# Eight early loads moved from step 4 to step 3, and two GpSimd copies moved behind a root

## The chip, the cores and the metric

The kernel runs on one core of a Trainium2 chip. The metric is the device time of one execution in microseconds (us). Times before the change come from three executions; one more execution was recorded by the hardware profiler. All places in time below are in us from the start of the profiled span.

## The reference, cut to what matters

Two decoder layers on `x` (16 sequences x 100 tokens x 256). Each sub-layer is added to the running rows:

```python
x = x + L0_attn(layernorm(x))              # a state-space mixer with an MLP      -> stage "mixer"
x = x + L0_xattn(layernorm(x), ctx, ctx)   # cross attention, 16 heads, 361 keys  -> stage "cross0"
x = x + L0_ffn(layernorm(x))               # 32 experts, 4 per token              -> stage "cross0"
x = x + L1_attn(layernorm(x))              # self attention                       -> stage "layer1"
x = x + L1_xattn(layernorm(x), ctx, ctx, mask)                                  # -> stage "layer1"
x = x + L1_ffn(layernorm(x))               # 8 experts, 1 per token               -> stage "experts1"
```

In the cross attention the queries are `(x Wq + bq)` and the keys `(ctx Wk + bk)`, split into 16 heads of 16. The kernel writes each of them as three bfloat16 parts (first, rest, third), so that a bfloat16 product of a stack of 96 rows keeps float32 precision.

## The kernel before

**Four stages with a barrier of all engines between them.** The first, `stage_mixer`, works in four steps, `n = 1` to `4`; a step holds four sequences. Beside the mixer and its MLP each step computes the key parts of both cross attentions for its four sequences: eight units, `u = 0` to `7`, with even `u` for layer 0. A unit is a projection on TensorE, a bias on ScalarE, and three parts by turns of ScalarE and VectorE; SyncE (SP) stores the parts to DRAM (`k_stack`, line 511). The queries of step `n - 1` are computed in step `n` and stored at `u == 6` (`store_queries`, line 487, `q_stack`). Those of step 4 are left to the next stage.

**The order on each engine is written out by hand.** Each engine has its own program of waits and instructions and runs it strictly in order. On SP, step `n` is: the stores of units 0 to 5, then `front(n + 1)`, the load of the next step's rows (line 474, into `mixer_xg`), then the stores of the queries, then units 6 and 7, then the store of the step's result (line 517, which waits for `v_out`). On VectorE the next step's `front` (two layer norms, lines 542 to 555) stands between the third part of unit 5 and the rest of unit 7, and the last thing in a step is the addition of the MLP's result (line 738), which increments `v_out`. TensorE waits for `v_out` and for the front's result before it turns the next step's rows (line 936).

**The first heads.** Cross attention starts with sequence 0. Its queries and keys are loaded ahead, during the mixer, by `first_heads` (lines 490 to 501): for each of two halves of the heads one load of queries (`ctx_first_q`) and three of keys (`ctx_first_k`), eight in all, on SP's queue. The semaphore of slot 0 of the key stores counts units 0 and 4 of every step.

**The start of the second stage,** `stage_cross_experts`. TensorE computes scores of sequence 0 (line 2579), VectorE takes their maxima (line 3026), and from then on TensorE works through sequences `b` and, in each, through twelve units `k`. Work of the queries of the mixer's step 4 is spread over `b == 0` and `b == 1`: VectorE's moments (lines 3198 to 3205) at `k == 0`, the inverse root on GpSimd (line 3375), VectorE's normalisation at `k == 4` (line 3210, four instructions, increments `q_norm`), TensorE's turn at `k == 6` and `7` (line 2714), which waits for `q_norm`. GpSimd first copies the selector rows of the keys (line 3365) into three buffers, then makes `base` for sequence 0 (line 3336), then the root, then `base` for sequence 1. TensorE waits for two of the three copies at `b == 2` and for all at `b == 3`.

Of the kernel before, what the change touches and what calls it, by code (L numbers as in the profile page):

```python
# [28 lines left out]
NG = B // G  # L29
# [3 lines left out]
KD = D // P  # L33
# [67 lines left out]
Q_PARTS = [(0, 0, 3), (1, 3, 5), (2, 5, 6)]  # L101
# [240 lines left out]
def stage_mixer(prog):  # L342
# [9 lines left out]
    UNITS = G * len(LAYERS)  # L352
    with stage(nc, "mixer") as (sem, sbuf, psum):
# [24 lines left out]
        keys_stored = [sem(f"keys_stored{s}") for s in range(4)]  # L378

        q_stats, q_mean, q_var, g_root, q_norm = (sem(n) for n in ("q_stats", "q_mean", "q_var", "g_root", "q_norm"))  # L380
        pe_qt, a_qt, pe_q, a_q, q_part1, q_rest_set, q_part2, q_part3, q_stored = (
            sem(n) for n in ("pe_qt", "a_qt", "pe_q", "a_q", "q_part1", "q_rest_set", "q_part2", "q_part3", "q_stored"))
# [49 lines left out]
        def out_rows(n):  # L432

            return prog.x2[:, (n - 1) * G:n * G, :] if n == NG else xo[:]
# [10 lines left out]
        def earlier(engine, semaphore, n, per=1):  # L445

            if not (isinstance(n, int) and n == 1):
                engine.wait_ge(semaphore, n * per - per)
# [17 lines left out]
        def group(dram, n):  # L466
            return dram[bass.ds((n - 1) * G, G)].rearrange("g t d -> t g d")

        with nc.Block() as block:
            @block.sync  # L470
            def _(sp):
                def front(n):
                    earlier(sp, x_free, n)
                    sp.dma_start(xg[:], group(x_dram, n)).then_inc(x_in, 16)
                    if n == 1:
                        prog.load_segment(sp, 0)
                        prog.load_segment(sp, 1)
                        prog.load_segment(sp, 2)
                        sp.dma_start(prog.consts[:], prog.ins["consts"]).then_inc(consts_in, 16)
                        prog.load_segment(sp, 3)  # L480

                def store_queries(n):
                    sp.wait_ge(q_part3, n)
                    for m in range(KD):
                        for k, at, end in Q_PARTS:
                            places = prog.q_stack[0][m, at:end, :, (n - 1) * G:n * G].rearrange("g p b t -> p g (b t)")
                            sp.dma_start(places, q_part[:, k, m].unsqueeze(1).broadcast_to(places.shape)
                                         ).then_inc(q_stored, 16)

                def first_heads():  # L490
                    sp.wait_ge(q_stored, (NG - 2) * KD * len(Q_PARTS) * 16)
                    sp.wait_ge(keys_stored[0], (NG - 1) * UNITS // 4 * 16)
                    for h in range(2):
                        sp.dma_start(prog.ctx_first_q[0:SHIFT_ROW, h, 0:HH * T].rearrange("p (h n) -> p h n", h=HH),
                                     prog.q_stack[0][h, :, :, 0:1].rearrange("g (d h) b t -> (g d) h (b t)", h=HH)
                                     ).then_inc(prog.ctx_first_in[h], 16)
                        for at, end in K_PARTS:
                            sp.dma_start(prog.ctx_first_k[at * DH:end * DH, h, 0:HH * S2]
                                         .rearrange("p (h n) -> p h n", h=HH),
                                         prog.k_stack[0][0, 0:end - at, :, h].rearrange("k (d h) n -> (k d) h n", h=HH)  # L500
                                         ).then_inc(prog.ctx_first_in[h], 16)

                def step(n, n_next):
                    if n == NG:
                        first_heads()
                    for u in range(UNITS):
                        if u == 6 and n > 1:
                            store_queries(n - 1)
                        layer, l = LAYERS[u % 2][0], u % 2
                        wait_unit(sp, v_part3, n, u)  # L510
                        sp.dma_start(prog.k_stack[layer][bass.ds(n * G + (u // 2 - G), 1)]
                                     .rearrange("b k p m n -> p (b k) (m n)"),
                                     part[u % 4][:].rearrange("p k m n -> p k (m n)")).then_inc(keys_stored[u % 4], 16)
                        if u == 5 and n_next is not None:
                            front(n_next)
                    sp.wait_ge(v_out, n)
                    sp.dma_start(group(out_dram, n), out_rows(n)).then_inc(out_stored, 16)

                run(sp, front, step)
                sp.wait_ge(q_stored, (NG - 1) * KD * len(Q_PARTS) * 16)  # L520
                sp.wait_ge(out_stored, 16 * NG)
                sp.wait_ge(rest_in, 16)
                sp.wait_ge(consts_in, 16)
                for s in range(4):
                    sp.wait_ge(keys_stored[s], B * len(LAYERS) // 4 * 16)
# [1740 lines left out]
def stage_cross_experts(prog):  # L2266
# [35 lines left out]
    with stage(nc, "cross0") as (sem, sbuf, psum):  # L2302
        def pair(label):
# [10 lines left out]
        consts_set, heads_set, third_heads_set = sem("consts_set"), sem("heads_set"), sem("third_heads_set")  # L2314
        q_stats, q_mean, q_var, g_root, q_norm = (sem(n) for n in ("q_stats", "q_mean", "q_var", "g_root", "q_norm"))
        pe_qt, a_qt, pe_q, a_q, q_part1, q_rest_set, q_part2, q_part3, q_stored = (
            sem(n) for n in ("pe_qt", "a_qt", "pe_q", "a_q", "q_part1", "q_rest_set", "q_part2", "q_part3", "q_stored"))
# [150 lines left out]
        with nc.Block() as block:  # L2468
# [862 lines left out]
            def _(g):  # L3331
# [32 lines left out]
                def select_heads(r, h):  # L3364
                    nc.gpsimd.tensor_copy(by_head(k_sb[r][:, h] if r < 2 else third_k, S2)[SHIFT_ROW:P],
                                          prog.c("head_sel")[SHIFT_ROW:P, h * HH:(h + 1) * HH].unsqueeze(2)
                                          .broadcast_to([32, HH, S2])).then_inc(third_heads_set, 1)

                for i, (r, h) in enumerate(((0, 0), (2, 1), (0, 1))):
                    select_heads(r, h)  # L3370
                    g.wait_ge(third_heads_set, i + 1)
                g.wait_ge(v_bias, 1)
                set_base(0)
                g.wait_ge(q_var, 1)
                nc.gpsimd.tensor_tensor(q_root[:], q_width[:], prog.half_neg[0:T, :], ALU.pow).then_inc(g_root, 1)
                g.wait_ge(g_root, 1)
                for b in range(B):
                    if b + 1 < B:
                        set_base(b + 1)
                    if b == 2 * G:  # L3380
                        g.wait_ge(zeroed, 16)
                    if b >= 2 * G:
                        scatter(b // G - 2, b % G * TOPK, TOPK // 2)
                    if b > 0:
                        root(b - 1)
                        inverse_length(b - 1)
                    if b >= 2 * G:
                        scatter(b // G - 2, b % G * TOPK + TOPK // 2, TOPK // 2)
# [267 lines left out]
```

## Time and profile before

| | |
|---|---|
| time, median of three | 1659.65 us (1657.05 to 1666.83) |
| the profiled execution: its own time | 1666.83 us |
| its span, first to last instruction | 1664.7 us |
| mean granted TensorE clock | 0.952 of full speed |
| mixer stage, about | 0 to 264 us of the span |
| second stage begins | 268.7 us |

The span and the profiled execution's own time differ by 2.1 us, which lies around the instructions. TensorE is busy for 89% of the span. The profile's rows of single engines in order of time give start, duration, engine and line, what is written from what, the number of instructions merged into the row, and in brackets the idle time before it with what ended it. SPq is the queue of SP: its rows are the issues of transfers, not the transfers.

### The profile page before, as it was taken

What the parts mean: (1) busy time and instruction counts of PE and PEld (TensorE: products, weight loads), DVE (VectorE), ACT (ScalarE), POOL (GpSimd) and SP (SyncE); (2) the same over time, 40 slices, a digit from 0 to 9 for tenths busy, and PEclk for the clock granted to TensorE, in tenths of its full rate; (3) what the DMA queues carried; (4) which work ended last, traced back from release to release, by engine and by line L of the source; (5) the groups of instructions that cost most, each with busy time, mean ns of one, the idle gap of its engine ahead of it and who ended that gap; (6) DMA issues with size and microseconds to landing.
All of it is one profiled execution on the core that took longest, in us unless ns stands there. A gap on an engine that the chain in (4) does not pass through costs nothing. (4 is left out here: it accounts for less than half of the span.)

```text
span 1664.7 us, 30297 instructions
## 1 busy us (share of the span) xinstructions
PE 1487.7 (89%) x11672; PEld 1119.9 (67%) x11672; DVE 790.6 (47%) x2238; ACT 701.7 (42%) x1473; POOL 479.4 (29%) x428
## 2 busy tenths in 40 slices
PE   6999997998888999999999957898799999939996
PEld 3666664666665668888888824565466667629885
DVE  6577574567765422222222246765566666541111
ACT  3464464666666112222222234456656555502221
POOL 2122122011334536666666420111111111012332
PEclk9999997999999999999999977999899999959998
DMA  7343556697772217777777527357477776339995
GB/s 300 121 146 97 159 163 111 122 171 125 127 132 60 61 40 196 201 199 194 196 195 195 137 48 168 85 111 148 93 143 128 122 134 120 67 110 328 325 297 151
DMA packets 252439, 250.86 MB, mean 151 GB/s; under 512 B 116724, under 2 KB 226700, under 8 KB 246796
## 3 DMA queue, kind: packets, MB, share of 16 engines
q1 hardware_dynamic: 210316, 221.13, 52.7%
q0 software_dynamic: 41984, 27.84, 9.9%
q8 instruction: 93, 1.52, 0.4%
q14 instruction: 46, 0.38, 0.1%
HBM read 194.10 MB, written 54.58 MB: 149 GB/s over the span
## 5 line engine op out<-in xcount | busy, mean ns | idle before, releaser
L2831 PE MATMUL cross_ps_score<-cross_q,cross_k 128*128 128x250 f32 x1024 | 223.5, 376 | 0.8 <-DVE cross_q L3312 0.8
L2831 PEld LDWEIGHTS cross_ps_score<-cross_q,cross_k 128*128 128x128 f32 x1024 | 195.5, 191 | 23.9 <-DVE cross_q L3312 1.0
L3321 DVE TENSOR_TENSOR cross_prob<-cross_act_,cross_ps_score 128x250 f32<-128x250 f32 x128 | 53.2, 416 | 268.3 <-ACT cross_act_ L2999 268.3
L3412 POOL DMA_INDIRECT x_sum<-cross_ye,cross_token x64 | 128.6, 2009 | 80.9 <-ACT cross_ye L3005 68.7
L1745 ACT ACTIVATE layer_parts<-layer_ps_prob 128x400 f32<-128x400 f32 (+1 forms) x192 | 97.0, 508 | 106.4 <-PE layer_ps_prob L1561 103.9
L3026 DVE TENSOR_REDUCE cross_nmax<-cross_ps_score 100x2 f32<-100x722 f32 x128 | 112.1, 903 | 61.8 <-PE cross_ps_score L2579 61.5
L2861 ACT ACTIVATE cross_prob<-cross_ps_prob 128x400 f32<-128x400 f32 (+1 forms) x192 | 96.3, 508 | 87.6 <-PE cross_ps_prob L2612 86.8
L2999 ACT ACTIVATE cross_act_<-cross_ps_score 128x250 f32<-128x250 f32 x128 | 48.6, 380 | 167.6 <-PE cross_ps_score L2831 167.6
L2843 PE MATMUL cross_ps_prob<-cross_val,cross_prob 128*125 128x256 f32 x512 | 115.8, 379 | 0.0
L3587 ACT ACTIVATE experts_h<-experts_ps_h,experts_b 128x128 f32<-128x128 f32 x160 | 45.7, 368 | 138.8 <-PE experts_ps_h L3556 138.8
L3402 POOL DMA_INDIRECT cross_xe<-ln_rows,cross_token x64 | 79.6, 1244 | 81.7 <-PE cross_ps_misc L2817 57.5
L2843 PEld LDWEIGHTS cross_ps_prob<-cross_val,cross_prob 128*125 128x125 f32 x512 | 93.5, 188 | 12.8
L928 PE MATMUL mixer_bank<-mixer_ctx,packed_sb 128*128 128x361 f32 x256 | 86.4, 481 | 2.5 <-ACT xt L832 2.2
L1967 DVE CUSTOM_DVE_ANT_0 packed_sb<-layer_ps_score,layer_mask 100x361 bf16<-100x361 f32 x128 | 63.0, 532 | 39.1 <-PE layer_ps_score L1518 38.7
L3005 ACT ACTIVATE cross_ye<-cross_ps_prob,cross_weight 125x256 f32<-125x256 f32 x64 | 26.9, 471 | 111.4 <-PE cross_ps_prob L2843 111.4
L1967 DVE CUSTOM_DVE_ANT_0 packed_sb<-layer_ring,layer_mask 100x361 bf16<-100x361 f32 x128 | 62.7, 528 | 22.7 <-PE layer_ring L1518 22.7
L3361 POOL DMA_INDIRECT row_token<-cross_choice,cross_row_put x64 | 64.3, 1005 | 31.6 <-issue 14.0
L928 PEld LDWEIGHTS mixer_bank<-mixer_ctx,packed_sb 128*128 128x128 f32 x256 | 48.8, 195 | 30.3 <-issue 5.3
L1556 PE MATMUL layer_ps_prob<-consts_sb,layer_mask 100*128 100x400 bf16 x192 | 64.5, 336 | 3.9 <-ACT layer_parts L1745 1.1
L813 ACT ACTIVATE mixer_full<-mixer_bank,packed_sb 128x361 f32<-128x361 f32 x64 | 34.8, 561 | 78.0 <-PE mixer_bank L928 76.2
L1561 PEld LDWEIGHTS layer_ps_prob<-layer_m_q,layer_stacks 128*128 128x128 bf16 x720 | 51.9, 98 | 23.1
L3522 POOL DMA_INDIRECT out<-experts_ye,experts_put x20 | 31.7, 1586 | 114.2 <-DMA out<-experts_ye,experts_put 103.2
(471 smaller groups left out, 3111.1 us busy)
## 6 DMA issues: line engine op xcount, KB each, us to landing
packed_sb<-in_w SPq DMA_DIRECT2D x20, 1024.0 KB, 7.0
experts_w<-in_w SPq DMA_DIRECT2D x20, 1024.0 KB
k_stack<-mixer_part SPq DMA_DIRECT2D x32, 541.5 KB, 3.9
cross_k<-in_wg SPq DMA_DIRECT2D x32, 512.0 KB, 5.4
cross_k<-in_wu SPq DMA_DIRECT2D x32, 512.0 KB, 6.9
cross_val<-in_wd SPq DMA_DIRECT2D x32, 512.0 KB, 5.2
layer_stacks<-k_stack SPq DMA_DIRECT2D x30, 270.8 KB, 5.3
cross_k<-k_stack SPq DMA_DIRECT2D x25, 270.8 KB
```

What stands on the lines that cost most here:

```text
L928: ins = nc.tensor.matmul(bank[6 + m][:, 0:S2], prog.w(f"{LAYERS[l][1]}_wk", KD)[:, k, m * P:(m + 1) * P], ctx[s][:, k, :], start=(k == 0), ...
L1556: nc.tensor.matmul(ps_prob[k % 2][:, 0:GT], mask[b % M_BUFFERS][:, at:at + P], prog.c("tile_diag")[0:T, :], start=True, stop=False)
L1745: nc.scalar.activation(m_prob_sb[0:rows_, q4 % 2, t, :], ps_prob[k % 2][0:rows_, 0:GT], ACT.Exp, scale=DH ** -0.5).then_inc(m_prob, 1)
L1967: ins = nc.vector.tensor_tensor_reduce(m_scratch[:, h % HH, :], m_score[(u % 2) * 2 + j][0:T, 0:S2], mask[b % M_BUFFERS][:, 0:S2], -1.0, - ...
L2831: ins = nc.tensor.matmul(ps_pre[m][:, side, 0:CAP], w[s][:, k, m * P:(m + 1) * P], xt[s][:, k, :], start=(k == 0), stop=(k == KD - 1))
L2843: ins = nc.tensor.matmul(ps_sum[s][0:HALF, t, :], up[s][:, m, t * HALF:(t + 1) * HALF], wd[s][:, m, :], start=(m == 0), stop=(m == NUP - 1))
L2861: nc.scalar.activation(prob[0:rows_, q4 % 2, t, :], ps_prob[k % 2][0:rows_, 0:GT], ACT.Exp, scale=DH ** -0.5).then_inc(a_prob, 1)
L3026: nc.vector.tensor_reduce(nmax[b % 2][:, 2 * u:2 * u + 2], ps_score[0:T, (u % 2) * 2:(u % 2) * 2 + 2, 0:S2], AX.X, ALU.max, negate=True).t ...
L3321: nc.vector.tensor_tensor(up[s][:, m, :], act_[:, m % 2, :], ps_pre[m][:, 1, 0:CAP], ALU.mult).then_inc(v_gated[m][s], 1)
L3361: g.indirect_dma_start(prog.row_token, bass.IndirectOffsetOnAxis(row_put[:, c:c + 1], 0), choice[:, c, :], None).then_inc(scattered, 16)
L3402: g.indirect_dma_start(xe[s][:, t, :], None, prog.ln_rows, bass.IndirectOffsetOnAxis(token[:, 2 * e + t:2 * e + t + 1], 0)).then_inc(rows_ ...
L3412: g.indirect_dma_start(prog.x_sum, bass.IndirectOffsetOnAxis(token[:, 2 * e + t:2 * e + t + 1], 0), ye[s][:, t, :], None, compute_op=ALU.a ...
```

## The change

It does two things. In the mixer, `first_heads` is called in step 3 right behind the store of unit 3, instead of at the beginning of step 4, and waits for smaller counts of the same two semaphores. In the second stage, GpSimd copies selector rows into one buffer before the root and into the two others behind it.

```diff
                 def first_heads():
-                    sp.wait_ge(q_stored, (NG - 2) * KD * len(Q_PARTS) * 16)
-                    sp.wait_ge(keys_stored[0], (NG - 1) * UNITS // 4 * 16)
+                    sp.wait_ge(q_stored, KD * len(Q_PARTS) * 16)
+                    sp.wait_ge(keys_stored[0], 5 * 16)
                     for h in range(2):
...
                 def step(n, n_next):
-                    if n == NG:
-                        first_heads()
                     for u in range(UNITS):
                         if u == 6 and n > 1:
                             store_queries(n - 1)
...
                         if u == 5 and n_next is not None:
                             front(n_next)
+                        if u == 3 and n == 3:
+                            first_heads()
...
-                for i, (r, h) in enumerate(((0, 0), (2, 1), (0, 1))):
-                    select_heads(r, h)
-                    g.wait_ge(third_heads_set, i + 1)
+                select_heads(0, 0)
+                g.wait_ge(third_heads_set, 1)
                 g.wait_ge(v_bias, 1)
                 set_base(0)
                 g.wait_ge(q_var, 1)
                 nc.gpsimd.tensor_tensor(q_root[:], q_width[:], prog.half_neg[0:T, :], ALU.pow).then_inc(g_root, 1)
                 g.wait_ge(g_root, 1)
+                select_heads(2, 1)
+                g.wait_ge(third_heads_set, 2)
+                select_heads(0, 1)
+                g.wait_ge(third_heads_set, 3)
                 for b in range(B):
```

## Rows read from the trace of the kernel before

**Rows 1.** The head of the page.
```profile
span 1664.7 us, 30297 instructions
```
**Rows 2.** In order of time, SP: the stores that end steps 2, 3 and 4.
```profile
141.91 0.30 SPq L517 DMA_DIRECT2D x_after<-mixer_xo  x1
...
202.40 0.30 SPq L517 DMA_DIRECT2D x_after<-mixer_xo  x1
...
262.88 0.30 SPq L517 DMA_DIRECT2D x_after<-packed_sb  x1
```
**Rows 3.** In order of time, SP: first and last of the eight loads, and the next store.
```profile
202.82 0.69 SPq L494 DMA_DIRECT2D ctx_first_q<-q_stack  x1
...
208.61 1.96 SPq L498 DMA_DIRECT2D ctx_first_k<-k_stack  x3
216.44 21.96 SPq L511 DMA_DIRECT2D k_stack<-mixer_part  x6
```
**Rows 4.** In order of time, SP, step 3: stores of units 2 and 3, and the row load.
```profile
169.81 2.02 SPq L511 DMA_DIRECT2D k_stack<-mixer_part  x2
...
177.97 0.42 SPq L474 DMA_DIRECT2D mixer_xg<-in_x  x1
```
**Rows 5.** In order of time, VectorE, step 3: front's start, last part, last addition.
```profile
183.67 1.41 DVE L542 BATCH_NORM_STATS2 mixer_stats<-mixer_xg 100x6 f32<-100x256 f32 x4 [5.23 <-DMA mixer_xg<-in_x]
...
195.97 0.91 DVE L537 TENSOR_TENSOR mixer_part<-mixer_rest,mixer_part 128x722 bf16<-128x722 f32 x1 [0.86 <-ACT mixer_part L825]
201.09 1.29 DVE L738 TENSOR_TENSOR mixer_xo<-mixer_bank,mixer_base 100x512 f32<-100x512 f32 x2 [4.21 <-PE mixer_bank L1023]
```
**Rows 6.** Stretches: length, busy PE, PEld, DVE, ACT, POOL, clock, DMA share, GB/s.
```profile
142.00:150.00 8.00, 7.97 (x36) 5.59 (x37) 4.60 (x8) 2.48 (x4) 0.00 (x0) 1.00 0.19 53
172.00:178.00 6.00, 6.00 (x19) 3.42 (x18) 4.28 (x6) 5.28 (x9) 0.60 (x1) 1.00 0.80 263
178.00:183.30 5.30, 5.30 (x18) 3.10 (x17) 0.44 (x1) 1.74 (x3) 0.00 (x0) 1.00 0.90 255
202.40:215.40 13.00, 12.88 (x55) 9.03 (x56) 9.23 (x21) 5.24 (x9) 1.40 (x2) 1.00 0.88 142
273.00:293.00 20.00, 16.66 (x126) 10.43 (x126) 14.74 (x39) 9.69 (x17) 6.22 (x5) 0.67 1.19 153
```
**Rows 7.** SP's issues at the second stage's start, and the landing time of one at 283.56.
```profile
269.56 0.58 SPq L2473 DMA_DIRECT2D cross_q<-q_stack  x1
...
276.90 0.59 SPq L2482 DMA_DIRECT2D cross_src<-in_ctx_t  x1
...
cross_src<-in_ctx_t SPq DMA_DIRECT2D x1, 361.0 KB, 11.2
```
**Rows 8.** In order of time, GpSimd (POOL): third copy, base 0, root, base 1.
```profile
274.08 2.59 POOL L3365 COPY cross_k<-consts_sb 32x2888 bf16<-32x2888 bf16 x1
279.56 0.73 POOL L3336 TENSOR_TENSOR cross_base<-cross_xin,cross_bias_sum 100x256 f32<-100x256 f32 x1 [2.89 <-issue]
284.30 1.01 POOL L3375 TENSOR_TENSOR cross_q_root<-cross_q_width,half_neg 100x4 f32<-100x4 f32 x1 [4.01 <-DVE cross_q_width L3205]
287.84 0.87 POOL L3336 TENSOR_TENSOR cross_base<-cross_xin,cross_bias_sum 100x256 f32<-100x256 f32 x1 [2.53 <-DMA cross_xin<-x_after]
```
**Rows 9.** VectorE's SBUF-to-SBUF instructions beside GpSimd's; base: min/median/max ns.
```profile
287.08 1.78 DVE L3210 TENSOR_SCALAR packed_sb<-packed_sb,cross_q_mv,cross_q_root 100x256 f32<-100x256 f32 x4
288.05 0.81 DVE L3210 TENSOR_SCALAR packed_sb<-packed_sb,cross_q_mv,cross_q_root 100x256 f32<-100x256 f32 x1
164.66 2.35 POOL L796 TENSOR_TENSOR mixer_base<-mixer_base,packed_sb 100x1024 f32<-100x1024 f32 x1
164.71 2.46 DVE L555 TENSOR_SCALAR mixer_xh<-mixer_x,mixer_mv,mixer_rstd 100x256 f32<-100x256 f32 x1 [0.93 <-POOL mixer_rstd L753]
L3336 POOL TENSOR_TENSOR cross_base<-cross_xin,cross_bias_sum x16: 725/728/867, 279.6 to 518.0; 100x256 f32<-100x256 f32 x16
```
**Rows 10.** In order of time, TensorE's turn of the queries; then a stretch, as in group 6.
```profile
288.92 0.93 PE L2714 MATMUL cross_ps_misc<-packed_sb 100*128 100x100 f32 x4 [1.43 <-DVE packed_sb L3210]
...
284.90:295.10 10.20, 8.77 (x83) 5.98 (x72) 6.91 (x11) 3.71 (x8) 1.28 (x2) 0.50 1.13 161
```

## The prediction

> **What bounds the kernel now.** I read the page first, then the two places that the change touches, each engine in order of time. The span is 1664.7 us [rows 1] and the profiled execution took 1666.83 us, so 2.1 us lie around it; it is the slowest of the three, 7.2 us above the median of 1659.65. My sum is a difference against this execution, and I put the difference on the median. A busy share for the whole span says nothing about 25 us of it. What counts is who waits last at four places: SP's queue at the start of step 4, the row load in step 3, GpSimd at the start of the second stage, and TensorE's wait for the normalised queries.
>
> **What the removal of the loads from step 4 is worth.** The eight loads are issued from 202.82 to 208.61 + 1.96 = 210.57, 7.75 us, and SP's next store is issued at 216.44 [rows 3], because its data comes only then. So SP has 5.9 us to spare, and nobody waits behind the loads. A second sign: the steps end at 141.91, 202.40 and 262.88 [rows 2]. Step 3, without the loads at its start, took 60.49 us, and step 4, with them, 60.48. The gain is 0. The transfers themselves lie in the stretch that ends at 215.4 [rows 6], and the first heads are first used when the second stage begins, at 268.7, so earlier data is worth 0 too.
>
> **What the insertion into step 3 costs.** The store of unit 3 is issued by 169.81 + 2.02 = 171.83 [rows 4]; the loads then stand before the stores of units 4 and 5 and, above all, before the load of the next step's rows, now issued at 177.97. Both new waits are met by then: the queries of step 1 were stored in step 2, and unit 0 of step 3 is stored before units 1 to 3. VectorE stands idle for 5.23 us for exactly this row load and starts at 183.67 [rows 5]. Any delay D of its landing moves the whole front. What hides it: VectorE's last part in this step ends at 195.97 + 0.91 = 196.88, and its next instruction waits 4.21 us for TensorE [rows 5]. Behind that wait the path is tight, since the addition releases the next step on TensorE. So the cost is D - 4.2 where D is over 4.2, and 0 otherwise.
>
> D by issue alone: with 7.75 us of issuing the loads end at 171.83 + 7.75 = 179.6, two stores follow, taken at the row load's 0.42 each [rows 4], and the row load goes out at 180.4, so D is at least 2.4.
>
> D by transfer work: I count a DMA share times its stretch. From 202.4 to 215.4 it is 13.0 x 0.88 = 11.4; the 400 KB store that opens that stretch costs 8.0 x 0.19 = 1.5 in the stretch where it is alone [rows 6]. The eight loads are therefore 9.9 us of work. In step 3 the DMA engines already do 6.0 x 0.80 + 5.3 x 0.90 = 9.6 from 172 until the rows have landed. Together 19.5. At a share of 1.0 this ends at 191.5, D = 8.2; at the 1.19 that these engines reach when they are full [rows 6], at 172 + 16.4 = 188.4, D = 5.1. I take the middle, D = 6.6: a cost of 2.4 us.
>
> The upper end comes from the second stage, where the same kind of load fills the engines. Eight half-loads there take 269.56 to 276.90, 7.3 us, and a 361 KB load issued behind them took 11.2 us to land [rows 7]. If our issuing stretches by 3 us and the landing takes 11.2, the rows land at 180.4 + 3 + 11.2 = 194.6, D = 11.3, a cost of 7.1. The lower end is 0.
>
> The Trainium skill says in "DMA: Bandwidth & Descriptors", section "Issuing engines are not separate DMA queues", that transfers of all issuing engines run on the same 16 DMA engines and interleave. By that, the stores and GpSimd's context load in the same stretch also compete with the row load, which is the assumption behind adding all work up; by issue alone the cost would be 0.
>
> **What the new order on GpSimd gives.** The third copy ends at 274.08 + 2.59 = 276.67, and GpSimd then waits 2.9 us before base 0, and 4.01 us on VectorE before the root [rows 8]. With one copy only it would be free some 5 us sooner and wait for the same two things. The gain is 0: neither base nor root comes earlier.
>
> **What the new order costs.** The two copies now start right behind the root, which ends at 284.30 + 1.01 = 285.31 [rows 8]. The first runs from about 285.4 to 288.0, the second would follow at once. VectorE's four instructions of the normalisation start at 287.08 [rows 9], in the middle of it. Three of them take 288.05 - 287.08 = 0.97 us, 0.32 each. The trace shows twice what happens when such an instruction meets a running GpSimd one. At 164.71 VectorE's took 2.46 us and ended at 167.17, just behind the GpSimd instruction of 164.66 to 167.01. At 288.05 the fourth took 0.81, while base 1 ran from 287.84 to 288.71 and was itself longer than its median of 0.73 [rows 8, 9]: GpSimd came in between the third and the fourth and made the fourth wait, although VectorE had more to do.
>
> So: the first waits until 288.0 and runs to 288.3. Then, as at 288.05, GpSimd's next instruction comes in, now a copy of 2.59 and not a base of 0.73, until 290.9. The other three end at 290.9 + 1.0 + 0.1 = 292.0. Today the normalisation ends at 287.08 + 1.78 = 288.86. The difference is 3.1 us. If VectorE keeps its turn and runs all four behind the first copy, they end at 289.4, a cost of 0.5. If the copies blocked nothing, base 1 would no longer be in the way, a gain of 0.4. I take 3.1, since the only row where a GpSimd instruction waits among these four shows it cutting in.
>
> Who waits: TensorE's turn of the queries starts at 288.92 after 1.43 us of idling for this very result [rows 10], and everything behind it on TensorE is in order. I see no later wait of that size in which the delay could vanish. Base 1, now about 4 us later, is needed only in sequence 1's result, and the copies only at `b == 2`, long after 291.
>
> The Trainium skill, in "SBUF — State Buffer", section "Who interferes with whom", says that GpSimd and a VectorE instruction that uses two ports hold a shared pair of ports exclusively for a whole instruction. The trace agrees, with 2.46 us instead of 0.4. It is the rule that speaks against this change; without it the second half would give the 0.4.
>
> **Sum.** 0 + 2.4 + 0 + 3.1 = +5.5 us. In the profiled execution's terms 1672.3, on the median 1659.65 + 5.5 = 1665.2 us. That is 0.33%, below the 0.5% (8.3 us) at which a measurement of this kernel can tell a difference.
>
> **The rivals.**
>
> A. Both delays are hidden. D stays under 4.2, since the rows' transfer work need not wait for all of the stores' work, and VectorE keeps its turn: 0 + 0.5, 1660.2 us. For it: D's floor by issue is 2.4. Against: 9.9 us of added work in a stretch already 80 to 90% full.
>
> B. The queue fills, and this ends on the slower side: the row load lands as slowly as the load of 11.2 us [rows 7]. It decides from D = 9.4, where 5.2 + 3.1 reaches 8.3. At D = 11.3 it is 7.1 + 3.1 = +10.2, 1669.9 us. Against it: in the second stage the queue had been full for much longer.
>
> C. TensorE's clock moves. From 284.9 to 295.1 it has 0.50 of full speed, 1.2 GHz, with 8.77 us busy [rows 10]; it fell after a stretch with pauses. If the rise stays where it is while the work moves 3.1 us later, 3.1 us of half-speed work run at full speed, a return of 1.5. If the longer pause adds a further half-speed stretch of like length, half of its 8.8 busy us are lost, 4.4. Against the sum: 1663.7, or 1669.6 us.
>
> D. The loads at step 4's start cost something that I don't see, a gain; rows 2 bound it at nothing, so only chance in clocks elsewhere could make it show.
>
> **How the numbers follow.** Both costs about as forecast, 1661.5 to 1668: 0.52. A: 0.23. B: 0.10. C: 0.11. D or a lucky set of clocks: 0.04. All of A, nearly all of the first and most of C lie within 0.5%. Slower by over 0.5% is B with a few points of C, of the first and of the scatter: 0.15. Faster: 0.04. Within: 0.81. The range runs from A less the scatter seen below the median, 2.6 us (1657.6, say 1658), to B's 1669.9 (1670).
>
> **What the profile after would show.** The eight loads issued from about 171.9; the row load of step 4 issued near 180 to 183, VectorE's wait for it about 12 us instead of 5.23; the end of step 3 not at 202.40 but near 204.8; step 4 again 60.5 long. In the second stage, counted from its start, one normalisation instruction of about 1.2 us and one of about 2.9, and TensorE's wait before its turn of 4.5 instead of 1.43. The prediction is wrong if step 3 keeps its 60.5 us, if the second copy waits until the four instructions are through, or if a later wait shrinks by what the turn was late.

## The result, and the profile after

| | before | changed |
|---|---|---|
| median of ten runs | 1662.80 us | 1671.86 us |
| lowest and highest | 1657.05, 1671.44 | 1668.22, 1685.03 |
| profiled execution, its span | 1666.83, 1664.7 | 1678.71, 1676.6 |
| mean granted clock | 0.952 | 0.953 |

The ratio over paired runs is 1.0069, 95% interval 1.0048 to 1.0092: slower by 0.69%, or 11.5 us (8.0 to 15.3). The two medians of ten differ by 9.1 us; over all 26 recorded executions of the changed kernel the median is 1674.9 us, 12.1 above 1662.80. The forecast was +5.5 us and 1665.2, with 1670 as the upper end.

**Step 3 of the mixer.** SP in order of time, from the end of step 2 to the end of step 4. SPq rows are issues.
```profile
142.06 0.30 SPq L517 DMA_DIRECT2D x_after<-mixer_xo  x1
156.10 15.88 SPq L509 DMA_DIRECT2D k_stack<-mixer_part  x4
172.09 0.69 SPq L494 DMA_DIRECT2D ctx_first_q<-q_stack  x1
172.83 3.07 SPq L498 DMA_DIRECT2D ctx_first_k<-k_stack  x3
175.94 0.77 SPq L494 DMA_DIRECT2D ctx_first_q<-q_stack  x1
176.75 3.07 SPq L498 DMA_DIRECT2D ctx_first_k<-k_stack  x3
179.86 1.48 SPq L509 DMA_DIRECT2D k_stack<-mixer_part  x2
181.38 0.81 SPq L474 DMA_DIRECT2D mixer_xg<-in_x  x1
...
205.76 0.30 SPq L517 DMA_DIRECT2D x_after<-mixer_xo  x1
...
267.93 0.30 SPq L517 DMA_DIRECT2D x_after<-packed_sb  x1
```
The eight loads stand where the four rows from 172.09 to 179.82 are. The row load goes out at 181.38 instead of 177.97 [rows 4]. Step 3 takes 205.76 - 142.06 = 63.70 us and step 4 62.17, against 60.49 and 60.48 [rows 2].

VectorE in order of time: the first part of `front`, its last part of the step, and the addition.
```profile
191.33 1.41 DVE L542 BATCH_NORM_STATS2 mixer_stats<-mixer_xg 100x6 f32<-100x256 f32 x4 [12.75 <-DMA mixer_xg<-in_x]
...
203.63 0.91 DVE L537 TENSOR_TENSOR mixer_part<-mixer_rest,mixer_part 128x722 bf16<-128x722 f32 x1 [0.86 <-ACT mixer_part L825]
204.46 1.28 DVE L738 TENSOR_TENSOR mixer_xo<-mixer_bank,mixer_base 100x512 f32<-100x512 f32 x2
```
The wait is 12.75 us where it was 5.23 [rows 5], so D is 7.5. The addition has no idle time ahead of it any more. The 4.21 us that covered the delay [rows 5] are used up, and the rest, 7.5 - 4.2 = 3.3, is what step 3 is longer by (3.2).

TensorE in order of time at the beginning of step 4, then two stretches in the columns of group 6.
```profile
205.88 0.88 PE L936 MATMUL mixer_bank<-packed_sb,mixer_xh 100*128 100x100 f32 x8 [3.48 <-DVE mixer_xo L738]
206.60 2.34 PE L928 MATMUL mixer_bank<-mixer_ctx,packed_sb 128*128 128x361 f32 x4
208.73 3.65 PE L971 MATMUL mixer_bank<-mixer_xt,packed_sb 128*128 128x400 f32 x8
```
```profile
206.90:210.30 3.40, 3.40 (x7) 1.91 (x6) 0.59 (x1) 1.88 (x3) 0.00 (x0) 0.50 0.50 139
295.70:302.50 6.80, 4.37 (x42) 3.22 (x43) 4.11 (x5) 1.49 (x3) 1.82 (x2) 0.50 0.55 71
```
TensorE stood idle for 3.48 us, and right behind it the granted clock is 0.50, 1.2 GHz instead of 2.4, for 3.40 us in which TensorE is busy throughout. Work of 3.4 us at half speed would take 1.7 at full speed, and 1.7 us is what step 4 is longer by. The forecast has nothing of this.

**The second stage.** It begins at 273.80, 5.05 us later. GpSimd, VectorE and TensorE in order of time. The four normalisation instructions stand first as one row and then one by one.
```profile
290.48 1.01 POOL L3374 TENSOR_TENSOR cross_q_root<-cross_q_width,half_neg 100x4 f32<-100x4 f32 x1 [5.15 <-DVE cross_q_width L3205]
291.56 2.59 POOL L3365 COPY packed_sb<-consts_sb 32x2888 bf16<-32x2888 bf16 x1
294.21 2.59 POOL L3365 COPY cross_k<-consts_sb 32x2888 bf16<-32x2888 bf16 x1
296.88 0.72 POOL L3336 TENSOR_TENSOR cross_base<-cross_xin,cross_bias_sum 100x256 f32<-100x256 f32 x1
```
```profile
292.74 5.34 DVE L3210 TENSOR_SCALAR packed_sb<-packed_sb,cross_q_mv,cross_q_root 100x256 f32<-100x256 f32 x4
292.74 1.56 DVE L3210 TENSOR_SCALAR packed_sb<-packed_sb,cross_q_mv,cross_q_root 100x256 f32<-100x256 f32 x1
294.22 2.73 DVE L3210 TENSOR_SCALAR packed_sb<-packed_sb,cross_q_mv,cross_q_root 100x256 f32<-100x256 f32 x1
296.88 0.88 DVE L3210 TENSOR_SCALAR packed_sb<-packed_sb,cross_q_mv,cross_q_root 100x256 f32<-100x256 f32 x1
297.68 0.40 DVE L3210 TENSOR_SCALAR packed_sb<-packed_sb,cross_q_mv,cross_q_root 100x256 f32<-100x256 f32 x1
```
```profile
298.13 0.93 PE L2714 MATMUL cross_ps_misc<-packed_sb 100*128 100x100 f32 x4 [5.37 <-DVE packed_sb L3210]
```
Lay the first two fences beside each other. The first normalisation waits for the end of the first copy (294.15), the second for the end of the second (296.80), the third for the end of base 1 (297.60); only the fourth has its own length. Each GpSimd instruction that is waiting comes in between two of VectorE's. Together they take 5.34 us, against 1.78 before [rows 9]. TensorE's wait is 5.37, against 1.43 [rows 10].

**The account.** TensorE's first product of sequence 1's probabilities starts at 310.61 in this profile and at 302.29 in that of before, 8.3 us later: 5.05 from the mixer and the rest from this wait, partly given back by the granted clock, which is 0.50 for 6.8 us at the place where it was 0.50 for 10.2 [rows 10]. The spans differ by 11.9 us. The largest further part is in the tenth to fifteenth sequences of the second stage, each of which is 0.6 to 2.6 us longer here, 6.5 together, of which shorter stretches elsewhere give back about 3. In the one that is 2.6 us longer TensorE's granted clock was 0.50 from 452.7 for 6.8 us, with 6.6 busy, and in the profile of before it was 1.00 throughout. What the rest is, is one of the questions of the experiments.

### The profile page after: what moved, and what is told of

It is laid out like the page before. It is cut to its first block and busy times, and to the rows that moved or that the text cites. A ratio compares the mean times of both kernels' runs of the same rounds, so it can differ in the third digit from the quotient of the medians.

```text
span 1676.6 us, 30297 instructions
## 1 busy us (share of the span) xinstructions
PE 1492.7 (89%) x11672; PEld 1122.4 (67%) x11672; DVE 793.3 (47%) x2238; ACT 701.1 (42%) x1473; POOL 480.3 (29%) x428
## 5 line engine op out<-in xcount | busy, mean ns | idle before, releaser
L928 PEld LDWEIGHTS mixer_bank<-mixer_ctx,packed_sb 128*128 128x128 f32 x256 | 49.8, 199 | 31.0 <-issue 6.5
```

Source lines behind the costliest of these rows:

```text
L928: ins = nc.tensor.matmul(bank[6 + m][:, 0:S2], prog.w(f"{LAYERS[l][1]}_wk", KD)[:, k, m * P:(m + 1) * P], ctx[s][:, k, :], start=(k == 0), ...
```

## The experiments

Every run is beside runs of the kernel before on the same chip. Their median was 1664.16 us in the group of the first four experiments (35 runs), 1672.11 in that of the next four (23 runs, another chip) and 1670.26 in a third group, a single run.

### e1: the loads alone

The eight loads in step 3 with the smaller counts, GpSimd's order as before.
```diff
+                        if u == 3 and n == 3:
+                            first_heads()
```


> The kernel before with the first half of the change alone: the eight loads behind unit 3's store in step 3; GpSimd's copies as before. Theory (row load late, then clock): VectorE waits about 12.7 us for the rows of step 4 as in the changed kernel, step 3 is 3.2 us longer than 60.5, TensorE stands idle for about 3.5 us before its turn and part of step 4 runs at half clock, 1.7 us more; the second stage begins 5.0 us late and its first sequence is as long as before. About +5 us in all. Rival (the two halves need each other, or the 9 us are scatter of the clock elsewhere): the second stage begins within 1 us of before, or it begins 5 us late and the time is nevertheless unchanged.

Measured: median 1671.30 us, ratio 1.0039 (1.0018 to 1.0061). VectorE's and TensorE's rows in order of time:
```profile
192.95 1.41 DVE L542 BATCH_NORM_STATS2 mixer_stats<-mixer_xg 100x6 f32<-100x256 f32 x4 [13.01 <-DMA mixer_xg<-in_x]
```
```profile
207.50 1.20 PE L936 MATMUL mixer_bank<-packed_sb,mixer_xh 100*128 100x100 f32 x8 [3.74 <-DVE mixer_xo L738]
```
Step 3 takes 63.96 us, step 4 62.15. Both parts of the mixer's loss come with the loads: 3.5 us by the late rows and 1.7 by the clock, which is at 0.50 from 207.9 for 3.4 us.

### e2: the copies alone

```diff
-                for i, (r, h) in enumerate(((0, 0), (2, 1), (0, 1))):
-                    select_heads(r, h)
-                    g.wait_ge(third_heads_set, i + 1)
+                select_heads(0, 0)
+                g.wait_ge(third_heads_set, 1)
...
+                select_heads(2, 1)
+                g.wait_ge(third_heads_set, 2)
+                select_heads(0, 1)
+                g.wait_ge(third_heads_set, 3)
```


> The kernel before with the second half of the change alone: two of GpSimd's copies behind the root; the eight loads as before. Theory (shared port): VectorE's four normalising instructions take about 5.3 us instead of 1.8, TensorE's wait before the turn of the queries is 4.5 to 5.4 us instead of 1.4, and sequence 1 begins 3 us late; mixer unchanged. About +3 us in all. Rival (a clock effect): the four instructions take 1.8 us and the time moves only by where TensorE's half-speed stretch falls. Open in both: whether the ten later sequences of the second stage get longer, as in the changed kernel (0.9 us each from the tenth on).

Measured: median 1668.38 us, ratio 1.0030 (1.0007 to 1.0053). All mixer steps take 60.5 us. TensorE in order of time:
```profile
293.81 0.93 PE L2714 MATMUL cross_ps_misc<-packed_sb 100*128 100x100 f32 x4 [5.36 <-DVE packed_sb L3210]
```
The same wait as in the whole change, without the loads; VectorE's four instructions take 5.36 us. From the first product of the second stage to TensorE's first product of sequence 1's probabilities it is 37.5 us here, and 36.8 and 36.0 in the two profiles of the changed kernel. In the nine profiles in which no late copy stands ahead of the normalisation and the moments are where they were, it is 31.4 to 33.5: the copies cost about 4 us there, and one profile alone can't tell that to better than 2, since the half-speed stretches of this stage fall differently from one execution to the next. The two parts add up: 0.39% + 0.30% is the 0.69% of the whole. Each has an interval of 0.2% to either side, so a sum that agrees to the hundredth is partly luck.

### e3 and e4: each half moved behind the instruction that it delays

e3 has the loads two units later, at `u == 5`, right behind the row load. e4 has the two copies wait for the normalisation.
```diff
+                        if u == 5 and n == 3:
+                            first_heads()
```
```diff
                 g.wait_ge(g_root, 1)
+                g.wait_ge(q_norm, 1)
+                select_heads(2, 1)
```


> As e1, but the eight loads stand in step 3 behind the load of the next step's rows (at unit 5) instead of ahead of it. Theory (the order on SP's queue is what costs): VectorE's wait for the rows is 5 to 6 us as before, step 3 is 60.5 us, the second stage begins within 0.5 us of before; no change in time. Rival (contention of the DMA engines, whatever the order): the rows still land 2 us or more late, since transfers of one queue interleave; with under 4.2 us of delay step 3 would still be 60.5 us, but the wait would show it.

> As e2, but the two late copies wait in addition until VectorE has normalised the queries. Theory (shared port): the four instructions take 1.3 us, 0.5 less than before, since base 1 is no longer in their way either; TensorE's wait before the turn is 0.9 to 1.4 us; time as before or 0.4 us less. Rival (any late copy costs, by base 1 coming late or by slowing other VectorE work): sequence 1 still begins 1 us or more late.

Measured: e3 median 1664.38 us, ratio 1.0001 (0.9976 to 1.0026); e4 1666.13 us, 1.0005 (0.9979 to 1.0031). VectorE in e3, then GpSimd, VectorE and TensorE in e4, each in order of time:
```profile
186.99 1.41 DVE L542 BATCH_NORM_STATS2 mixer_stats<-mixer_xg 100x6 f32<-100x256 f32 x4 [6.40 <-DMA mixer_xg<-in_x]
```
```profile
291.11 2.59 POOL L3365 COPY packed_sb<-consts_sb 32x2888 bf16<-32x2888 bf16 x1 [2.71 <-DVE packed_sb L3210]
```
```profile
289.60 1.38 DVE L3210 TENSOR_SCALAR packed_sb<-packed_sb,cross_q_mv,cross_q_root 100x256 f32<-100x256 f32 x4
```
```profile
291.03 0.56 PE L2714 MATMUL cross_ps_misc<-packed_sb 100*128 100x100 f32 x4 [1.37 <-DVE packed_sb L3210]
```
The same transfers in the same step, issued behind the row load, delay it by 1.2 us (6.40 against 5.23; the five other profiles with this part of the mixer unchanged have 5.22 to 5.59, so every D here is good to about 0.4), and the idle time ahead of the addition hides that: steps 3 and 4 take 60.5. The same copies behind the normalisation leave it at 1.38 us. So it is neither the work that costs nor the stage it stands in, but what it stands ahead of. The removals are worth nothing that can be measured: e3 has the loads gone from step 4, which takes 60.47 us against 60.48, and e4 has GpSimd free before the root, with 33.3 us to sequence 1's first product against 33.5 and 33.2 in the two profiles of before. Their times alone say it only to within 4 us.

### e7 and e11: half of the loads

In e7 the four loads of one half stand ahead of the row load, those of the other right behind it. In e11 the other half stays in step 4.
```diff
+                def first_heads(h):
...
+                        if n == 3 and u in (3, 5):
+                            first_heads(u // 4)
```
```diff
                     if n == NG:
-                        first_heads()
+                        first_heads(1)
...
+                        if n == 3 and u == 3:
+                            first_heads(0)
```


> As e1, but only the four loads of the first half stand behind unit 3's store in step 3; the other four stand behind the load of the next step's rows. Theory (the delay of the rows is proportional to the work put ahead of them, and 4.2 us of it are hidden): VectorE waits 5.3 + 3.8 = 9.1 us, step 3 is 60.5 us, step 4 too; time as before. Rival (a fixed cost of the interruption, or no threshold): step 3 is 1 to 3 us longer than 60.5.

> As e7, but the second half's four loads stay at the beginning of step 4 instead of behind the row load of step 3. In e7 the wait for the rows was 10.6 us and step 3 61.5, over the threshold. Theory (work ahead of the rows and work issued right behind them both delay them; behind them all eight cost 1.0 us in e3): the wait is 9.2 to 9.7 us, the rows are at most 4.2 us late, step 3 is 60.5 us. Rival (four loads ahead of the rows are enough to cost): step 3 is 61.3 to 61.6 us as in e7.

Measured: e7 median 1674.70 us, ratio 1.0021 (1.0001 to 1.0041); e11 a single execution, 1678.65 us. VectorE in e7 and in e11, then SP in e11:
```profile
190.39 1.41 DVE L541 BATCH_NORM_STATS2 mixer_stats<-mixer_xg 100x6 f32<-100x256 f32 x4 [10.60 <-DMA mixer_xg<-in_x]
```
```profile
188.96 1.41 DVE L543 BATCH_NORM_STATS2 mixer_stats<-mixer_xg 100x6 f32<-100x256 f32 x4 [8.95 <-DMA mixer_xg<-in_x]
```
```profile
143.49 0.30 SPq L518 DMA_DIRECT2D x_after<-mixer_xo  x1
...
179.55 0.47 SPq L474 DMA_DIRECT2D mixer_xg<-in_x  x1
```
I had expected e7 to keep its 60.5 us, and it did not: D is 10.60 - 5.23 = 5.4 and step 3 takes 61.54. Beside e11 this shows that what follows the row load in the queue delays it too; I had counted only what stands ahead. e11 takes that away: D is 3.7, half of the whole's 7.5, and step 3 takes 60.49. In e11 the row load is issued 179.55 - 143.49 = 36.06 us into the step, as in the kernel before (177.97 - 141.91) [rows 2, 4], and in e7 36.04. So there its issue is not late at all: the whole D of 3.7 is transfers that share the DMA engines, and only in the changed kernel does a later issue (39.32) come on top. Four values of D now lie on one line, with the lengthening D - 4.3 above 4.3 and nothing below:

| | D | step 3 longer by |
|---|---|---|
| e3, all behind | 1.2 | 0.0 |
| e11, half ahead | 3.7 | 0.0 |
| e7, half ahead, half behind | 5.4 | 1.1 |
| the changed kernel | 7.5 | 3.2 |

The other four profiles with all eight loads ahead have D of 6.8, 7.2, 7.5 and 7.8 and lengthenings of 2.5, 2.9, 3.2 and 3.5, on the same line.

e11's 1678.65 us is a single execution, 8.4 above the single one beside it, with no longer step in the mixer; the 23 executions of the kernel before in the second group alone spread over 15.5 us, so it says nothing.

### e6 and e10: the idle time of TensorE filled

To separate the late rows from the clock, TensorE gets products to do at the beginning of step 4, ahead of the instruction that waits. The added work goes into a bank that nobody reads; the rest is e1.
```diff
+                    if n == 4:
+                        wait_half(pe, a_key, n, 0, 1, 1)
+                        for _ in range(9):
+                            nc.tensor.matmul(bank[7][:, 0:S2], prog.w("x0_wk", KD)[:, 0, P:2 * P],
+                                             ctx[0][:, 0, :], start=True, stop=True)
```
e10 has `range(4)` in its place.

> As e1 (eight loads in step 3 ahead of the rows), and in step 4 TensorE runs nine products of 128x361 float32 into a free bank, whose result nobody reads, in the place where it stood idle for 3.5 us. They add work and leave none out. Theory (the longer idle time lets the clock fall): with the idle time filled to under 1 us, TensorE keeps its full clock and step 4 is 60.5 us instead of 62.15; step 3 stays at about 63.8; the second stage begins 1.65 us earlier than in e1. Rival (the extra 1.65 us of step 4 have another cause, for instance late stores or the transfers still under way): step 4 stays at 62.1.

> e6 with four added products instead of nine: each product ran as two instructions of 0.31 us, so that nine took 5.6 us and outran the idle time by 2.2 us. Four take 2.5 us. The products add work and leave none out. Theory (the 1.7 us of step 4 in e1 and in the first profile of the changed kernel are a half-speed stretch after the long idle time): no half-speed stretch near 207 to 212, step 4 at most 60.6 us, step 3 between 62.9 and 64.0. Rival (another cause): step 4 is 62.1 us although the idle time is filled. The second profile of the changed kernel, with 2.7 us of idle time, had no such stretch, so one look without it is weaker evidence than one with it.

Measured: e6 median 1684.49 us, ratio 1.0080 (1.0049 to 1.0112). It was mis-sized: the nine products run as 18 instructions of 0.31 us, 5.62 in all, and last 2.1 us longer than the wait that they were to fill, so that step 4 becomes longer by the experiment itself (62.63). Its trace has no low clock at that place, but its time decides nothing, and what it has beyond e1's cost and these 2.1 us is left open. e10 is a single execution (1674.22 us). TensorE in order of time; the first row is the four added products, as eight instructions:
```profile
201.91 2.59 PE L967 MATMUL mixer_bank<-mixer_ctx,packed_sb 128*128 128x361 f32 x8
205.50 0.88 PE L936 MATMUL mixer_bank<-packed_sb,mixer_xh 100*128 100x100 f32 x8 [0.99 <-DVE mixer_xo L738]
206.21 1.41 PE L928 MATMUL mixer_bank<-mixer_ctx,packed_sb 128*128 128x361 f32 x4
207.45 2.85 PE L976 MATMUL mixer_bank<-mixer_xt,packed_sb 128*128 128x400 f32 x8
```
Step 3 is as long as with the change, 63.64 us, since the rows are as late (12.70). The idle time is 0.99 instead of some 3.5, no half-speed stretch follows, the same eight products take 2.85 us instead of 3.65, and step 4 takes 60.47. So the 1.7 us of step 4 are the clock's: they come and go with the half-speed stretch. In e6 and e10 the rows are late and the idle time is filled, and no such stretch follows; this speaks for the idle time as what lets the clock fall, and against the late rows as such. With two profiles filled, and one unfilled without the stretch (below), it is not more than that.

### e8: one copy behind the root

```diff
-                for i, (r, h) in enumerate(((0, 0), (2, 1), (0, 1))):
-                    select_heads(r, h)
-                    g.wait_ge(third_heads_set, i + 1)
+                select_heads(0, 0)
+                g.wait_ge(third_heads_set, 1)
+                select_heads(2, 1)
+                g.wait_ge(third_heads_set, 2)
...
+                select_heads(0, 1)
+                g.wait_ge(third_heads_set, 3)
```


> As e2, but only one of the copies stands behind the root, the other ahead of it. Theory (each GpSimd instruction that waits cuts in between two of VectorE's four, in turn): the first of the four is held until the copy ends, about 1.6 us, base 1 then cuts in once, about 0.9 us, the last two take 0.4 each; together about 2.8 us, and TensorE waits about 2.8 us instead of 1.4 or 5.4. Rival (the cost is that of late copies as such, each the half of the 4.0 us): TensorE waits 3.4 us; or (VectorE keeps its turn once it has it) the four take 2.4 us with no second long one.

Measured (a single execution, 1677.39 us): VectorE's four together, then the first and the second as a row each and the third and fourth in one, then GpSimd, each in order of time.
```profile
287.98 3.05 DVE L3210 TENSOR_SCALAR packed_sb<-packed_sb,cross_q_mv,cross_q_root 100x256 f32<-100x256 f32 x4
287.98 1.60 DVE L3210 TENSOR_SCALAR packed_sb<-packed_sb,cross_q_mv,cross_q_root 100x256 f32<-100x256 f32 x1
289.50 0.88 DVE L3210 TENSOR_SCALAR packed_sb<-packed_sb,cross_q_mv,cross_q_root 100x256 f32<-100x256 f32 x1
290.30 0.73 DVE L3210 TENSOR_SCALAR packed_sb<-packed_sb,cross_q_mv,cross_q_root 100x256 f32<-100x256 f32 x2
```
```profile
286.84 2.59 POOL L3365 COPY cross_k<-consts_sb 32x2888 bf16<-32x2888 bf16 x1
289.50 0.72 POOL L3336 TENSOR_TENSOR cross_base<-cross_xin,cross_bias_sum 100x256 f32<-100x256 f32 x1
```
3.05 us against the 2.8 expected, and TensorE waits 3.04. The first waits out the copy (to 289.43), the second waits out base 1 (to 290.22), the third and fourth are free. Each late copy has its own price: 1.4 with none of them, 3.05 with one, 5.35 with two, and each step is no more than the instruction that came in.

### The two kernels again

> The changed kernel once more, one look. It is here for its profile: if the longer sequences 10 to 15 of the first profile of it (0.7 to 2.6 us each) come from the change, they are there again; if they are chance, which e1 and e2, whose profiles don't have them, and the sum of their ratios (0.39% + 0.30% = 0.69%) speak for, they are gone. Steps 3 and 4 again 63.7 and 62.2 us, TensorE's wait before the turn again 5.4.

> The kernel before once more, one look. Theory (sequences 10 to 15 are 0.8 to 1 us longer each on the chip of one group of runs, whatever the kernel, and not on the other's): its sequences 10 to 15 are either like those of its first profile or like those of the changed kernel's, and the same as those of the three kernels run beside it. Rival: they differ within this group of runs from kernel to kernel. Steps 3 and 4 60.5 us, TensorE's wait 1.4 us.

Measured: the changed kernel again 1675.13 us (span 1673.0), the kernel before again 1670.95 (span 1668.8). TensorE in order of time in the first, at the beginning of step 4:
```profile
204.40 0.88 PE L936 MATMUL mixer_bank<-packed_sb,mixer_xh 100*128 100x100 f32 x8 [2.72 <-DVE mixer_xo L738]
```
Here TensorE was idle for 2.72 us, the clock did not fall, and step 4 took 60.48. So the 1.7 us are not in every execution of the changed kernel; of the three profiles with all eight loads ahead and nothing filled in, two have them, after 3.48 and 3.74 us of idling. How often they come over all executions is not known. The rows were also a little earlier here, with D at 6.8 and step 3 at 62.94 us. VectorE's and TensorE's rows of the second stage are the same as in the first profile (5.35 and 5.38 us).

The kernel before shows what sequences 10 to 15 are. GpSimd makes base once in every sequence. The first and the last of four such rows in a line, three sequences apart, in the first profile of the kernel before and in the second (third group):
```profile
471.15 0.73 POOL L3336 TENSOR_TENSOR cross_base<-cross_xin,cross_bias_sum 100x256 f32<-100x256 f32 x1 [7.85 <-DVE packed_sb L3050]
...
518.03 0.74 POOL L3336 TENSOR_TENSOR cross_base<-cross_xin,cross_bias_sum 100x256 f32<-100x256 f32 x1 [7.65 <-DVE packed_sb L3050]
```
```profile
470.84 0.73 POOL L3336 TENSOR_TENSOR cross_base<-cross_xin,cross_bias_sum 100x256 f32<-100x256 f32 x1 [8.51 <-DVE packed_sb L3050]
...
522.32 0.74 POOL L3336 TENSOR_TENSOR cross_base<-cross_xin,cross_bias_sum 100x256 f32<-100x256 f32 x1 [9.14 <-DVE packed_sb L3050]
```
Three sequences take 518.03 - 471.15 = 46.9 us in the one and 51.5 in the other, with not a line changed. In the second TensorE's granted clock was 0.50 for 6.8 us within them; e10, from the same group and without such a stretch, takes 49.8, so some 1.7 us of the difference are the clock's. In all eight profiles of the second and third groups these sequences are long, in all four of the first they are short. From the eleventh of these rows to the sixteenth it is 80.1 us in the profiles of the first group and 84.5 to 84.6 in those of the others without a half-speed stretch. The trace shows where this lies: GpSimd's pause before its inverse length (line 3351) is 1.1 to 1.3 us in all these sequences of the first group's profiles and of the first profile of before. In each long profile it is 2.2 to 2.4 in four of them, and over the five sequences that is 10.3 us of pause in e10 against 5.8 in the first profile of before: the whole 4.5 us. The first profile of the changed kernel has the long pauses too. Over the six sequences in question its pauses are 12.1 us, against 6.9 before. They and the half-speed stretch cover the 6.5 us by which these sequences were longer. The pauses are no effect of the change, since the second profile of the kernel before has them too. What lengthens the pause in those chips or sessions was not found; the profile names nothing that GpSimd waits for there. On which chips the first two profiles were taken is not on record.

### e9: a version that takes the wait away

If TensorE's wait for the normalisation is a cost also in the kernel before (1.43 us), earlier moments should take it away: moments ahead of the loop over `b`, normalisation at `k == 3`, GpSimd and the loads as before.
```diff
-    Q_NORMAL_AT, Q_TURN_AT, Q_PROJECT_AT = 4, (6, 7), (9, 11)
+    Q_NORMAL_AT, Q_TURN_AT, Q_PROJECT_AT = 3, (6, 7), (9, 11)
...
+                query_moments()
...
-                        if b == 0 and k == 0:
-                            query_moments()
```


> A try for a version faster than the kernel before: loads and copies as before, but VectorE takes the moments of the queries before the first maxima of sequence 1 and normalises one unit earlier. Theory (TensorE's wait of 1.4 us for the normalised queries is on the path): that wait falls under 0.3 us and sequence 1 begins 1.2 us earlier; in the time this is 0.07%, too little to be told from no change. Rival: the wait moves to VectorE's maxima or the clock stretch, and sequence 1 begins no earlier.

Measured: median 1669.80 us, ratio 0.9988 (0.9968 to 1.0009). TensorE in order of time:
```profile
287.10 0.93 PE L2714 MATMUL cross_ps_misc<-packed_sb 100*128 100x100 f32 x4
```
The wait is gone from the trace, and sequence 1's first product comes 29.8 us after the stage's first, at least 1.5 us earlier than in the nine profiles of 31.4 to 33.5. In the time the gain, if there is one, is below what the measurement can tell. No version was found that is measurably faster than the kernel before.

## Why the prediction was wrong

**The removals: right.** Both were costed at 0. e3 and e4, which keep each removal without the harm, come out at 1.0001 and 1.0005, and step 4 without the loads is as long as before.

**The loads in step 3: right in mechanism, a term too small.** "By transfer work" gave a middle of D = 6.6 between 5.1 and 8.2, and a cost of 2.4. D is 7.5 in the changed kernel, and step 3 is longer by 3.2 (2.5 to 3.5 over the profiles of the change, e1 and e10). The issue took 7.73 us, as forecast (7.75). The slack of 4.2 was right: by the table under e11 it is 4.3. Where the middle went wrong, the changed kernel's stretch from 172 to the landing shows, in the columns of group 6:
```profile
172.00:191.20 19.20, 19.20 (x67) 11.92 (x66) 4.86 (x6) 9.30 (x16) 0.60 (x1) 1.00 1.07 241
```
The share, 1.07, is what the middle implies (19.5 us of work in the 18.3 until VectorE's start at 183.7 + 6.6 is 1.07; the prediction counted D from the landing at 183.3, which makes it 1.09). The work is not: 19.2 x 1.07 = 20.5 us, 1.0 more than the 19.5 counted, and 1.0 / 1.07 is the missing 0.9 of D. Why is argued, not shown: I had counted up to the old landing what else the engines do, and a load that lands later also shares them with what is issued behind it in the meantime, as the four loads behind it do in e7.

**The copies: right in mechanism, a term too small.** I took GpSimd's next instruction to cut in between two of VectorE's, from the one row where that happened [rows 8, 9], and it did, in every profile with the late copies. I had it cut in once and set the end 3.1 us later. It cuts in each time that it has something waiting, and base 1 does as a third, so that the four take 5.34 us, 3.6 more than the 1.78 of rows 9, and 4.0 more than the 1.37 that they take in the second profile of before, where base 1 ran ahead of them. The Trainium skill ("SBUF — State Buffer", section "Who interferes with whom") has the exclusive hold of the shared ports for a whole instruction, with which these rows agree (1.56, 2.73 and 0.88 us against 0.40); the order in which the two engines come to hold them is shown here by the rows alone.

**The step that failed as a difference is the sum,** "0 + 2.4 + 0 + 3.1 = +5.5": it has no term for the clock. Rival C had one, but put it at the second stage, where the clock is already low [rows 10]. It came at the start of step 4: TensorE's idling for D - 4.2 was counted once, as time, and it costs a second time where the clock falls behind it, 1.7 us in two of three profiles. With the terms as measured the sum is 3.2 + 1.7 + 3.6 = 8.5 us; TensorE's start of sequence 1 is later by 8.3, the medians differ by 9.1. Of the 3.0 us that were missing, the clock is 1.7, the loads 0.8 and the copies 0.5. At 11.5 (8.0 to 15.3) the paired ratio asks for more than the traces locate, and the difference of some 3 us is within its interval; it stays open whether there is anything in it. The prediction gave 0.81 to a change of under 0.5%; 0.69% (0.48 to 0.92) is outside.

**The step that failed as a time is the base,** "on the median 1659.65 + 5.5 = 1665.2". I put the difference on the median of three executions; the median of ten is 1662.80. Of the 6.7 us between 1665.2 and 1671.86 the base is 3.15, more than the error of any term of the sum. On 1662.80 the forecast would have been 1668.3 and the upper end, which came from rival B's +10.2, 1673.0: the range would have held the result, though by the price of a queue that did not fill.

**The rivals.** A is out: D was well over 4.2, and VectorE did not keep its turn. B's direction is right and its price is not: D did not come near 11.3. The 11.2 us that it used belong to a load issued at 283.56 [rows 7], with six more loads between it and the eight; the load of the same size right behind the eight, at 276.90, took 9.7. C is right that the clock moves and wrong in the place: in the second stage the half-speed stretch is shorter than before, 6.8 us against 10.2.

## What to carry to other kernels

- A transfer or copy that is "free" because its engine idles costs what stands behind it in the same queue. Ask what its next neighbour on the queue is for: the same loads cost 0.39% ahead of the row load and nothing measurable behind it, the same copies 0.30% ahead of the normalisation and nothing measurable behind it.
- When a delay exceeds its cover, price TensorE's idle time twice: as time, and as the half-speed stretch that can follow. Here it followed in two of three profiles.
- Put a difference on a median of more than three runs when the spread of the runs is as large as the difference, and look in the kernel before for the stretches that vary from chip to chip before a difference of two spans is explained.

## What the runs showed of the hardware that was not expected

- A waiting GpSimd instruction was let in after each of VectorE's normalisation instructions, although VectorE had more to do: four of 0.32 to 0.40 us took 1.38 us with none in the way, 3.05 with two, 5.34 with three.
- At the start of step 4 an idle time of TensorE of 3.48 and 3.74 us was followed by 3.4 us at 1.2 GHz; one of 2.72, of 1.33 and of 0.99 was followed by none.
- Loads behind a load on the same queue delay it too, without its issue being late: about 1 us by eight, and four ahead with four behind make 5.4 where four ahead alone make 3.7.
- The same unchanged kernel takes 46.9 us for three sequences in one profile and 51.5 in another: some 1.7 by a half-speed stretch, the rest by a longer pause of GpSimd (2.2 to 2.4 us where it was 1.1 to 1.3) that goes with the chip or the session.
